# A four-layer recurrent kernel on one core: low-rank and decay products in row and column groups of TensorE, a new order of the pieces, an earlier copy of the values, and a transpose mode

## The chip, the cores and the metric

The kernel runs on one core of one Trainium2 chip. The metric is the device time of one execution in microseconds (us), the median over runs. One profiled execution of the kernel before is shown beside it.

## The reference, cut to what matters

Four layers follow each other. The first three are recurrent layers over 4 sequences of 512 tokens with 512 channels (32 heads of 16); the fourth is an attention over a context of 1024 tokens, which the change does not touch. One recurrent layer computes:

```
xa  = layernorm(x);  sx = shifted(xa) - xa
xxx = tanh((xa + sx*maa_x) @ maa_w1)          # 512 -> 5 streams x 32
xxx = einsum(xxx, maa_w2)                     # each stream: 32 -> 512   ("low-rank products")
xm  = xa + sx*(maa_stack + xxx)               # five mixtures: k, w, v, r, g
w   = exp(-exp(time_decay + tanh(xw @ td_w1) @ td_w2))   # 512 -> 64 -> 512  ("decay products")
r, k, v = xr @ Wr.T, xk @ Wk.T, xv @ Wv.T;  g = silu(xg @ Wg.T)
per token: out = r*(u*k*v + s);  s = k*v + w*s            # 16 x 16 state per head
out = groupnorm(out) * g;  x1 = x + out @ Wo.T
xc  = layernorm(x1); rr = sigmoid(xr2 @ Wfr.T); kk = relu(xk2 @ Wfk.T)**2
x   = x1 + rr * (kk @ Wfv.T)
```

## The kernel before

All values are float32, channels lie on partitions (4 tiles of 128), tokens on the free axis. A unit is one sequence and one half of it: 256 tokens. Each layer has 8 units, so there are 24. The work of a unit is cut in four parts that run in four successive steps: part n (first layernorm, low-rank products, mixtures, projections), part b (the recurrence), part c (output projection, second layernorm) and part e (feed-forward). In step s the engines do part n of unit s+1, b of unit s, c of unit s-1 and e of unit s-2. So there are 27 steps, from -1 to 25. Steps 0 to 22 have both part n and part b, step -1 has only part n, step 23 has b, c and e but no n.

The recurrence works in leaves of 8 tokens. In a leaf, products of pairs of tokens are summed over the channels of a head by a matmul with a block matrix (pieces P0a, P0b, P1, P2a, P2b, P4a to P4d), multiplied by values on VectorE and gathered in o_leaf. Between leaves a scan on VectorE (`scan`) runs over the states; the state updates k x v come from TensorE in 32 x 32 tiles (`updates`, pieces U00 to U13) from keys and values that were turned to lie by token (`keys_by_token` KT0/KT1, `values_by_token` VT0/VT1). The values are then copied by DMA to v_m, spread out for the updates: `load_vm`, four DMAs for pair 0 of the head groups, four for pair 1, in one buffer. The outputs of the states are products in 128 x 32 tiles (`outputs`, `rz` times `s_bd`), added in PSUM to the leaf's own outputs, which `own_outputs` turns (by a matmul with the identity).

Every engine is in order, and its order is written out by hand: one list of calls for each engine and step, which must agree with the lists of PSUM tiles (`A_TILES`, `B_TILES`, `C_TILES`), since a ring of PSUM banks is filled and emptied in that order. The A ring (part n) has three banks, the B ring (part b) two, the outputs one, the C ring (parts c and e) two. A tile can be opened when the tile three (two) places earlier in its ring is emptied by ScalarE or VectorE. SyncE issues `load_vm`, the loads of x and the stores, GpSimd the weights (eight of 1 MB a unit, three slots), each in one fixed order too.

In part n, `lora` computes the five 32-wide streams (a 128-column and a 32-column product), ScalarE takes tanh into th (w, v, r, g in partition groups 0 to 3) and thk (k alone). `lora_pair` issues two streams' products together: each has a contraction of 32 partitions, each its own row group and its own PSUM bank. `lora_k` issues the third stream's alone. `decay_in` and `decay_out` are the two decay products, with 64 output columns and 64 contraction rows. VectorE's `mixing` turns each low-rank product into a mixture with two multiply-adds of 256 tokens, and one addition at its end (mix_w, mix_v, mix_k, mix_r, mix_g). `project` is one half of a 512 x 512 projection: 8 matmuls of 128 x 128 by 256 tokens. Each float32 matmul appears as two records of TensorE in the trace, a transpose as one.

Of the kernel before, what the change touches and what calls it, by code (L numbers as in the profile page):

```python
# [39 lines left out]
W1_AT, W2_AT, W2K_AT, TD1_AT, TD2_AT, SMALL = 0, 640, 1152, 1664, 1920, 2432  # L40
# [7 lines left out]
ROWS_OF = {"w": 0, "v": 1, "r": 2, "g": 3}  # L48
# [45 lines left out]
def other_tiles():  # L94
# [15 lines left out]
A_TILES = [("s1", "act"), ("m1", "dve"), ("s2", "act"), ("i1", "dve"), ("w1", "act"), ("w2w0", "dve"), ("w2v0", "dve"), ("w2w1", "dve"),  # L110
           ("w2v1", "dve"), ("td1", "act"), ("v0", "act"), ("w2k0", "dve"), ("w2k1", "dve"), ("td2_0", "act"), ("td2_1", "act"), ("v1",
           "act"), ("w2r0", "dve"), ("w2g0", "dve"), ("w2r1", "dve"), ("w2g1", "dve"), ("r0", "act"), ("k0", "act"), ("k1", "act"), ("r1",
           "act"), ("g0", "act"), ("g1", "act")]
B_TILES = [("P0a", "dve"), ("P0b", "dve"), ("P1", "dve"), ("P2a", "dve"), ("VT0", "act"), ("VT1", "act"), ("P2b", "dve"), ("P4a", "dve"),
           ("P4b", "dve"), ("P4c", "dve"), ("KT0", "act"), ("KT1", "act"), ("U00", "act"), ("P4d", "dve"), ("U01", "act"), ("U02", "act"),
# [3 lines left out]
C_TILES = [(2, "fr0", "act"), (2, "fk0", "act"), (2, "fk1", "act"), (2, "fr1", "act"), (1, "wo0", "dve"), (2, "fv0", "dve"), (1, "wo1",  # L119
# [5 lines left out]
LEAF_DVE = ["p0", "p1", "u1w", "u1r", "u1k", "p2a", "p2b", "u2w", "u2r", "u2k", "o1", "o2a", "p4a", "p4b", "p4c", "p4d", "u8", "u4r", "u4k",  # L125
# [13 lines left out]
def laid_out():  # L139
# [15 lines left out]
    for i, name in enumerate(("th", "thk", "tdh", "st_a")):  # L155
        at[name] = (at["lm"][0] + TC * i, TC)
# [94 lines left out]
def build(nc, a):  # L251
    ctx = ExitStack()
    with ctx:
# [41 lines left out]
        w2k = small_w[:, W2K_AT:W2K_AT + E]  # L295
# [10 lines left out]
        th, thk, tdh = part_of("th"), part_of("thk"), part_of("tdh")  # L306
# [59 lines left out]
        for _s in range(-1, ITS + 2):  # L366
            weights += [(_it, n) for _it, n in ((_s - 2, WFR), (_s - 2, WFK), (_s - 1, WO), (_s - 2, WFV),
                                                (_s + 1, WV), (_s + 1, WR), (_s + 1, WK), (_s + 1, WG)) if 0 <= _it < ITS]
# [79 lines left out]
        def _(sp):  # L448
# [39 lines left out]
            for s in range(ITS + 2):  # L488
# [3 lines left out]
                if 1 <= n < ITS - 1:  # L492
                    load_xl(n + 1)
                if e >= 0:
                    store_x(e)
                if 0 < b < ITS:
                    load_x1(b)
                if b < ITS:
                    load_vm(b, 1)
                if n < ITS and n % UNITS_PER_LAYER == UNITS_PER_LAYER - 1 and n + 1 < ITS:  # L500
                    sp.wait_ge(a_ring.full, a_ring.full_at(n, "w2g1"))
# [78 lines left out]
        def _(pe):  # L580
# [68 lines left out]
            def lora_k(it):  # L649
                for n in range(2):  # L650
                    t = opened(a_ring, it, f"w2k{n}")
                    for o in range(2):
                        m = 2 * n + o
                        last = mm(t[:, o * TC:(o + 1) * TC], w2k[0:DM, P * m:P * m + P], thk[0:DM, :], start=True, stop=True, skip_group_check=True)
                    a_ring.fill(last, it, f"w2k{n}")

            def lora_pair(it, one, two, n):

                pe.wait_ge(*a_ring.empty_at(it, "w1"))
                t = [opened(a_ring, it, f"w2{s}{n}") for s in (one, two)]  # L660
# [7 lines left out]

            def mixed(it, s):
                return mix[(STREAMS * it + ORDER.index(s)) % 3]  # L670

            def decay_in(it):
                pe.wait_ge(a_dve.sem, a_dve.at(it, "mix_w"))
                t = opened(a_ring, it, "td1")
                for k in range(KT):
                    last = mm(t[0:DD, 0:TC], td1[:, k, :], mixed(it, "w")[:, k, :], start=k == 0, stop=k == KT - 1)  # L676
                a_ring.fill(last, it, "td1")

            def decay_out(it):
                pe.wait_ge(*a_ring.empty_at(it, "td1"))  # L680
                for n in range(2):
                    t = opened(a_ring, it, f"td2_{n}")
                    for o in range(2):
                        m = 2 * n + o
                        last = mm(t[:, o * TC:(o + 1) * TC], td2[0:DD, P * m:P * m + P], tdh[0:DD, :], start=True, stop=True, skip_group_check=True)
                    a_ring.fill(last, it, f"td2_{n}")
# [58 lines left out]
            def own_outputs(it, pair):  # L745
                t = opened(o_ring, it, f"O{pair}").rearrange("p (k s c) -> p k s c", k=2, s=2)
                pe.wait_ge(leaf.sem, leaf.at(it, "o4d"))
                for i in range(2):
                    for s in range(2):
                        mm(t[:, i, s, :], tokens(o_leaf[:, 2 * pair + i, :], s), ident[:], start=i == 0 and s == 0, stop=False, skip_group_check=True)  # L750
# [40 lines left out]
            for s in range(-1, ITS + 2):  # L791
# [5 lines left out]
                if has_b:  # L797
                    products(b, "P0a")
                if 0 < n and has_n:
                    norm_a(n, "s1")  # L800
                if has_b:
                    products(b, "P0b")
                    products(b, "P1")
                if has_e:
                    feed(e, "fk", 1)
                if has_b:
                    products(b, "P2a")
                if 0 < n and has_n:
                    norm_a(n, "m1")
                if has_e:  # L810
                    feed(e, "fr", 1)
                if has_b:
                    values_by_token(b)
                if 0 < n and has_n:
                    norm_a(n, "s2")
                if has_b:
                    products(b, "P2b")
# [4 lines left out]
                if 0 < n and has_n:  # L822
                    norm_a(n, "i1")
                if has_b:
                    products(b, "P4b")
                    products(b, "P4c")
# [1024 lines left out]
```

## Time and profile before

| | us |
|---|---|
| median of 3 runs (3674.37 to 3686.33) | 3674.67 |
| the profiled execution's own time | 3682.92 |
| its span | 3681.2 |
| recurrent part, up to its last product on TensorE | 2635.8 |
| one full step | 102.90 |

The page gives TensorE busy for 94% of the span, VectorE for 72%, ScalarE for 51%. TensorE's busy digit is 9 in every slice from the 4th to the 27th of 40, which is the recurrent part after its first steps. The granted clock is 0.966 of full speed over the whole span. Rows of the trace that follow read: start in us, duration in us, engine and line, xcount for instructions merged into one row, and in brackets the idle time before it and who ended it.

### The profile page before, as it was taken

How to read it: one execution, taken by the hardware profiler on the slowest of the kernel's cores; microseconds unless marked ns; L12 is line 12 of the kernel's file. 1: busy time of each engine (PE TensorE's matmuls, PEld its weight loads, DVE VectorE, ACT ScalarE, POOL GpSimd, SP SyncE). 2: the span in 40 equal slices, each digit the busy share in tenths (PEclk: the TensorE clock that was granted, in tenths of full speed). 3: DMA queues.
4: the chain of work that ended last, by engine and by line, in shares of the span. 5: the costliest groups of instructions: out<-in, count | busy, mean ns of one | idle time of the engine just before them, and what ended most of it. 6: DMA issues, size and time to landing. Idle time of an engine off the chain costs nothing.

```text
span 3681.2 us, 74341 instructions
## 1 busy us (share of the span) xinstructions
PE 3449.4 (94%) x31664; PEld 2579.3 (70%) x31664; DVE 2645.1 (72%) x3721; ACT 1878.6 (51%) x2991; POOL 109.5 (3%) x204
## 2 busy tenths in 40 slices
PE   6889999999999999999999999997588898997998
PEld 4667777777777777777777777775446565565666
DVE  2778887888788888887888888876137466566466
ACT  1455545555555555555555455554146455555555
POOL 1000000000000000000000000000000000000000
PEclk8899999999999999999999999998799899999999
DMA  3113322223233223223233223221323214133222
GB/s 112 44 59 115 115 95 98 99 104 115 87 110 115 104 90 115 98 103 111 86 114 115 104 90 113 101 84 64 139 58 80 83 47 105 47 73 90 48 70 57
DMA packets 91912, 336.61 MB, mean 91 GB/s; under 512 B 16705, under 2 KB 37825, under 8 KB 65601
## 3 DMA queue, kind: packets, MB, share of 16 engines
q0 software_dynamic: 27648, 201.34, 15.1%
q1 hardware_dynamic: 63936, 130.52, 12.3%
q8 instruction: 253, 4.15, 0.5%
q14 instruction: 75, 0.61, 0.1%
HBM read 252.11 MB, written 16.78 MB: 73 GB/s over the span
## 4 chain that ended last, share of the span: by engine, by line
PE 82%; DVE 8%; ACT 3%; SPq 2%; issue 2%; DMA 2%; POOL 0%; ACTq 0%; DVEq 0%; POOLq 0%
PE psum L695 35%; PE psum L704 5%; PE psum L764 4%; PE psum L964 4%; PE psum L741 3%; PE psum L940 3%; PE psum L930 3%; PE psum L665 3%; PE psum L982 2%; PE psum L954 2%; SPq L547 2%; DVE rw L1531 2%; PE psum L945 2%; PE psum L936 2%; PE psum L676 1%
## 5 line engine op out<-in xcount | busy, mean ns | idle before, releaser
L695 PE MATMUL psum<-rw 128*128 128x256 f32 x6144 | 1429.4, 389 | 12.0 <-DVE rw L1369 7.2
L695 PEld LDWEIGHTS psum<-rw 128*128 128x128 f32 x6144 | 1174.8, 194 | 245.6 <-issue 75.2
L1531 DVE TENSOR_TENSOR rw<-rw 128x2048 f32<-128x2048 f32 x192 | 432.6, 2286 | 11.7 <-PE psum L764 11.1
L1707 DVE CUSTOM_DVE_ANT_0 psum<-psum,mem 128x1024 f32<-128x1024 f32 x256 | 313.5, 1225 | 113.9 <-PE psum L954 113.8
L1295 ACT ACTIVATE rest<-psum,mem 128x1024 f32<-128x1024 f32 x256 | 285.0, 1113 | 72.4 <-DVE mem L1707 70.5
L1414 DVE SCALAR_TENSOR_TENSOR rw<-psum,rw 128x256 f32<-128x256 f32 x480 | 199.2, 477 | 153.1 <-PE psum L665 98.6
L1084 ACT ACTIVATE rw<-psum 128x512 f32<-128x512 f32 x192 | 111.8, 595 | 328.6 <-PE psum L695 328.4
L964 PE MATMUL psum<-ident,rest 128*128 128x128 f32 x2048 | 273.2, 277 | 4.0 <-DVE mem L1677 3.8
L1122 ACT ACTIVATE rw<-psum 128x512 f32<-128x512 f32 x192 | 202.1, 1137 | 130.1 <-PE psum L741 128.4
L964 PEld LDWEIGHTS psum<-ident,rest 128*128 128x128 f32 x2048 | 237.4, 142 | 44.1 <-issue 13.5
L954 PE MATMUL psum<-side 128*128 128x512 f32 x512 | 212.0, 495 | 30.2 <-ACT rest L1295 22.7
L704 PE MATMUL psum<-rw 128*128 128x512 f32 x432 | 227.8, 628 | 7.2 <-DVE rw L1447 5.8
L1288 ACT ACTIVATE mem<-psum 128x512 f32<-128x512 f32 x256 | 151.9, 594 | 159.7 <-PE psum L964 159.7
L1501 DVE TENSOR_TENSOR rw<-psum,rw 128x512 f32<-128x512 f32 x168 | 113.5, 687 | 159.6 <-PE psum L704 159.6
L1514 DVE TENSOR_TENSOR_SCAN rw<-rw 128x2112 f32<-128x2112 f32 x48 | 218.5, 4552 | 6.1 <-ACT rw L1122 6.1
L764 PE MATMUL psum<-rw 128*32 128x128 f32 x6144 | 197.4, 278 | 7.0 <-DVE rw L1531 7.0
L1712 DVE COPY mem<-psum 128x512 f32<-128x512 f32 x256 | 175.9, 687 | 36.5 <-PE psum L964 36.4
L1139 ACT ACTIVATE rw<-rw 128x1024 f32<-128x1024 f32 x96 | 192.8, 2010 | 0.0
L764 PEld LDWEIGHTS psum<-rw 128*32 128x32 f32 x6144 | 163.5, 111 | 38.0 <-issue 23.1
L1022 ACT ACTIVATE rw<-rw 128x256 f32<-128x256 f32 x192 | 99.7, 590 | 164.0 <-DVE rw L1364 164.0
L1785 POOL DMA_DIRECT2D rw<-big_dram x192 | 101.0, 528 | 2488.9 <-PE psum L695 2486.2
L741 PE MATMUL psum<-rw 32*32 32x128 f32 x6144 | 167.0, 274 | 6.2 <-DMA rw<-rw 4.6
(147 smaller groups left out, 4503.9 us busy)
## 6 DMA issues: line engine op xcount, KB each, us to landing
rw<-big_dram POOLq DMA_DIRECT2D x192, 1024.0 KB, 5.1
side<-mem SPq DMA_DIRECT2D x256, 128.0 KB, 2.4
rw<-xs_dram SPq DMA_DIRECT2D x32, 512.0 KB, 3.4
side<-mem SPq DMA_DIRECT2D x256, 64.0 KB, 2.0
rw<-rw SPq DMA_DIRECT2D x192, 64.0 KB, 3.1
xs_dram<-rw SPq DMA_DIRECT2D x24, 512.0 KB, 2.7
rw<-x_dram SPq DMA_DIRECT2D x16, 512.0 KB, 3.8
mem<-ctx_dram SPq DMA_DIRECT2D x4, 2048.0 KB, 7.9
```

What stands on the lines that cost most here:

```text
L695: last = mm(t[:, o * TC:(o + 1) * TC], big[:, k, P * m:P * m + P], src[:, k, 0:TC], start=k == 0, stop=k == KT - 1, skip_group_check=True)
L704: b_ring.fill(mm(t, blk, src, start=True, stop=True), it, name)
L741: last = mm(t[32 * g:32 * g + 32, k, :, :, s], k_t[rows, s, 256 * pair + at:256 * pair + at + 32], v_m[rows, s, :, at:at + 32], start=True ...
L764: last = mm(t[32 * q:32 * q + 32, o, s, :], rz[:, k, c, 32 * m:32 * m + 32], s_bd[:, half, NM * i + m, :], start=False, stop=c == 3, skip_ ...
L954: last = mm(t[:, sh, :], q_side[group % 2][:, h, P * q:P * q + P].bitcast(F32R), k_side[group % 2][:, h, sh * 512:sh * 512 + 512].bitcast( ...
L964: last = nc.tensor.transpose(tokens(t, o), tokens(probs[:, n % HPT, :], first + o), ident[:])
L1122: b_ring.empty(f(to, t, ACT.Copy), it, f"U{pair}{q}")
L1295: s_ring.empty(f(probs[:, n % HPT, :].rearrange("p (a s) -> p a s", a=2), s_ring.bank(n, "s"), ACT.Exp, scale=-1.0, bias=mx[:, n % 8:n % 8 ...
L1414: last = stt(to[:, m, :], t[:, o * TC:(o + 1) * TC], par(layer, MAAS, KT * FAN[s] + m), sxa[:, m, :], ALU.add, ALU.mult)
L1514: state_dve.inc(nc.vector.tensor_tensor_scan(s_flat, d_flat, s_flat, 0.0, ALU.mult, ALU.add), it, f"scan{pair}")
L1531: state_dve.inc(tt(s_bd[:, half, :, :].rearrange("p c (h j) -> p c h j", h=4), own, place, ALU.mult), it, f"b{k}{half}")
L1707: maxima.inc(nc.vector.tensor_tensor_reduce(t, t, mbias.rearrange("p (a s) -> p a s", a=2), 1.0, 3.4e38, ALU.add, ALU.min, accum_out=mx[:, ...
```

## The change

It has six parts.

1. Low-rank products: streams w, v and k are issued together in three row groups (`lora_three`), two calls of 6 matmuls; r and g together in two (`lora_two`), two calls of 4. `lora_k` is gone. The stream alone in a tile of its own is now g (thg), not k.
2. Decay: `decay_in` computes the two halves of 128 tokens in two column groups of 64, one bank; `decay_out` computes them in two row groups of 64, a bank each, since td2's rows now lie twice in small_w. ScalarE's exponentials read 8 pieces of 128 tokens where they read 4 of 256.
3. `own_outputs` sets is_transpose on its four matmuls.
4. The order of the pieces on TensorE, VectorE and ScalarE, with the rings' lists.
5. `load_vm` of pair 1 stands ahead of the store of x (`store_x`) and the load of x1 on SyncE.
6. The weights' order is V, K, R, G instead of V, R, K, G; the reload of small_w at a layer's end waits for td2_1 as well.

```diff
-A_TILES = [... ("w1", "act"), ("w2w0", "dve"), ("w2v0", "dve"), ("w2w1", "dve"),
-           ("w2v1", "dve"), ("td1", "act"), ("v0", "act"), ("w2k0", "dve"), ("w2k1", "dve"), ("td2_0", "act"), ("td2_1", "act"), ("v1",
+A_TILES = [... ("w1", "act"), ("w2w0", "dve"), ("w2v0", "dve"), ("w2k0", "dve"),
+           ("w2w1", "dve"), ("w2v1", "dve"), ("w2k1", "dve"), ("v0", "act"), ("td1", "act"), ("v1", "act"), ("td2_0", "act"), ("td2_1",
...
+                if b < ITS:
+                    load_vm(b, 1)
                 if e >= 0:
                     store_x(e)
                 if 0 < b < ITS:
                     load_x1(b)
-                if b < ITS:
-                    load_vm(b, 1)
...
+            def lora_three(it, n):
+                if n == 0:
+                    pe.wait_ge(*a_ring.empty_at(it, "w1"))
+                t = [opened(a_ring, it, f"w2{s}{n}") for s in "wvk"]
                 for o in range(2):
                     m = 2 * n + o
-                    for i, s in enumerate((one, two)):
+                    for i, s in enumerate("wvk"):
                         rows = slice(DM * ROWS_OF[s], DM * ROWS_OF[s] + DM)
                         last = mm(t[i][:, o * TC:(o + 1) * TC], w2[rows, P * m:P * m + P], th[rows, :], ...)
...
             def decay_in(it):
                 for k in range(KT):
-                    last = mm(t[0:DD, 0:TC], td1[:, k, :], mixed(it, "w")[:, k, :], ...)
+                    for h in range(2):
+                        last = mm(t[DD * h:DD * h + DD, 0:P], td1[:, k, :], tokens(mixed(it, "w")[:, k, :], h), ...)
             def decay_out(it):
-                        last = mm(t[:, o * TC:(o + 1) * TC], td2[0:DD, P * m:P * m + P], tdh[0:DD, :], ...)
+                t = [opened(a_ring, it, f"td2_{h}") for h in range(2)]
+                for m in range(KT):
+                    for h in range(2):
+                        rows = slice(DD * h, DD * h + DD)
+                        last = mm(t[h][:, P * m:P * m + P], td2[rows, P * m:P * m + P], tdh[rows, 0:P], ...)
...
-                        mm(t[:, i, s, :], tokens(o_leaf[:, 2 * pair + i, :], s), ident[:], start=i == 0 and s == 0, stop=False, ...)
+                        mm(t[:, i, s, :], tokens(o_leaf[:, 2 * pair + i, :], s), ident[:], start=i == 0 and s == 0, stop=False, is_transpose=True, ...)
...
             def decay_out(it):                                  # ScalarE
-                for n in range(2):
-                    for o in range(2):
-                        last = f(hm["w"][:, 2 * n + o, :], t[:, o * TC:(o + 1) * TC], ACT.Exp, bias=par(layer, TDEC, 2 * n + o))
+                for h in range(2):
+                    for m in range(KT):
+                        last = f(tokens(hm["w"][:, m, :], h), t[:, P * m:P * m + P], ACT.Exp, bias=par(layer, TDEC, m))
```

TensorE's new order in one step, in the names of the calls (o is `own_outputs`, out is `outputs`, U `updates`): fr0 fk0 P0a P0b s1 VT m1 P1 P2a fr1 P2b s2 wo0 P4a i1 fk1 P4b wo1 P4c lora P4d fv0 KT three0 c.s1 o0 U00 U01 three1 U02 U03 fv1 v0 U10 c.m1 U11 decay_in v1 out00 decay_out out01 U12 two0 U13 k0 two1 out10 c.s2 out11 k1 r0 o1 out20 out21 c.i1 r1 out30 out31 g0 g1 N0 N1.

On TensorE, in the middle of part n of a full step, before (L741 updates, L665 `lora_pair`, L676 and L685 decay, L654 `lora_k`, L695 projections):

```order
L665 MATMUL psum<-rw 128x256 x3
L741 MATMUL psum<-rw 32x4x32 [waits b_ring_dve]
L741 MATMUL psum<-rw 32x4x32 x15
L741 MATMUL psum<-rw 32x4x32 [waits b_ring_act]
L741 MATMUL psum<-rw 32x4x32 x15
L695 MATMUL psum<-rw 128x256 [waits c_ring_dve,slot_loaded1,f_act]
L695 MATMUL psum<-rw 128x256 x7
L676 MATMUL psum<-rw 64x256 [waits a_ring_dve,a_dve]
L676 MATMUL psum<-rw 64x256 x3
L695 MATMUL psum<-rw 128x256 [waits a_ring_dve,slot_loaded2,a_dve]
L695 MATMUL psum<-rw 128x256 x7
L654 MATMUL psum<-rw 128x256 [waits a_ring_dve]
```

The same place of the changed kernel (L750 updates, L659 `lora_three`, L683 and L693 decay, L704 projections, L773 outputs, L620 the second norm's mean):

```order
L659 MATMUL psum<-rw 128x256 x5
L750 MATMUL psum<-rw 32x4x32 [waits b_ring_act]
L750 MATMUL psum<-rw 32x4x32 x15
L750 MATMUL psum<-rw 32x4x32 [waits b_ring_act]
L750 MATMUL psum<-rw 32x4x32 x15
L704 MATMUL psum<-rw 128x256 [waits c_ring_dve,slot_loaded1,f_act]
L704 MATMUL psum<-rw 128x256 x7
L704 MATMUL psum<-rw 128x256 [waits a_ring_dve,slot_loaded2,a_dve]
L704 MATMUL psum<-rw 128x256 x7
L750 MATMUL psum<-rw 32x4x32 [waits b_ring_act,vm_loaded]
L750 MATMUL psum<-rw 32x4x32 x15
L620 MATMUL psum<-rw 128x256 [waits c_ring_act]
```

The first value projection v0 now follows fv1 directly, the first update of pair 1 (which waits for vm_loaded) comes right behind it, and the decay products come later, with 8 matmuls of 128 tokens each.

On SyncE in an early step before (L483 `load_vm`, L463 load of x for part n, L473 `store_x`, L469 load of x1):

```order
L483 DMA rw<-rw 32x2x256 [waits b_ring_full,b_ring_act]
L483 DMA rw<-rw 32x2x256 x3
L463 DMA rw<-x_dram 128x1024 [waits a_act]
L473 DMA xs_dram<-rw 128x1024 [waits f_dve]
L469 DMA rw<-x_dram 128x1024 [waits x_stored]
L483 DMA rw<-rw 32x2x256 [waits b_ring_full]
L483 DMA rw<-rw 32x2x256 x3
```

and in the changed kernel:

```order
L483 DMA rw<-rw 32x2x256 [waits b_ring_full,b_ring_act]
L483 DMA rw<-rw 32x2x256 x3
L463 DMA rw<-x_dram 128x1024 [waits a_act]
L483 DMA rw<-rw 32x2x256 [waits b_ring_full]
L483 DMA rw<-rw 32x2x256 x3
L473 DMA xs_dram<-rw 128x1024 [waits f_dve]
L469 DMA rw<-x_dram 128x1024 [waits x_stored]
```

The four copies of pair 1 no longer stand behind the store, which waits for VectorE (f_dve), and behind the load that waits for that store.

## Rows read from the trace of the kernel before

**Rows 1.** The page, part 1: busy time, share and instructions of each engine.

```profile
PE 3449.4 (94%) x31664; PEld 2579.3 (70%) x31664; DVE 2645.1 (72%) x3721; ACT 1878.6 (51%) x2991; POOL 109.5 (3%) x204
```

**Rows 2.** Windows: stretch, its length, busy us of each engine, clock, DMA.

```profile
1404.97:1507.87 102.90, 102.68 (x999) 80.58 (x999) 85.52 (x112) 55.35 (x84) 4.20 (x8) 1.00 0.29 103
```

**Rows 3.** Chain that ended last, one full step: start us, us to next.

```profile
1415.65 0.95 PE psum L750 x8
1416.60 1.88 PE psum L764 x64
...
1450.44 0.87 PE psum L718 x8
1451.32 0.58 PE psum L603 x32
...
1452.96 3.45 PE psum L695 x16
1456.41 0.86 PE psum L704 x2
1457.27 0.84 PE psum L608 x8
...
1471.23 1.01 PE psum L741 x32
...
1473.29 1.06 PE psum L665 x8
...
1476.99 1.49 PE psum L741 x64
1478.49 3.65 PE psum L695 x16
1482.14 1.87 PE psum L676 x8
...
1487.66 1.92 PE psum L654 x8
1489.58 1.92 PE psum L685 x8
...
1496.21 1.09 PE psum L750 x8
```

**Rows 4.** Timeline of VectorE in the same step.

```profile
1429.57 3.25 DVE L1369 SCALAR_TENSOR_TENSOR rw<-rw 128x256 f32<-128x256 f32 x8
...
1473.33 0.69 DVE L1501 TENSOR_TENSOR rw<-psum,rw 128x512 f32<-128x512 f32 x1 [5.64 <-PE psum L704]
...
1477.03 1.66 DVE L1414 SCALAR_TENSOR_TENSOR rw<-psum,rw 128x256 f32<-128x256 f32 x4 [0.88 <-PE psum L665]
1478.60 2.35 DVE L1419 TENSOR_TENSOR rw<-rw 128x1024 f32<-128x1024 f32 x2
1480.87 4.55 DVE L1514 TENSOR_TENSOR_SCAN rw<-rw 128x2112 f32<-128x2112 f32 x1
...
1491.69 4.49 DVE L1531 TENSOR_TENSOR rw<-rw 128x2048 f32<-128x2048 f32 x2
```

**Rows 5.** Timeline of ScalarE: a copy of states, and the decay's exponentials.

```profile
1488.19 1.98 ACT L1139 ACTIVATE rw<-rw 128x1024 f32<-128x1024 f32 x1
1490.73 1.64 ACT L1066 ACTIVATE rw<-psum,rw 128x256 f32<-128x256 f32 x4 [0.57 <-PE psum L685]
```

**Rows 6.** Timeline of SyncE's queue in the same step.

```profile
1487.35 0.33 SPq L473 DMA_DIRECT2D xs_dram<-rw  x1
1490.01 0.32 SPq L469 DMA_DIRECT2D rw<-xs_dram  x1
1490.38 2.52 SPq L483 DMA_DIRECT2D rw<-rw  x4
```

**Rows 7.** The page, part 6: the copies of `load_vm`, count, KB each, us to landing.

```profile
rw<-rw SPq DMA_DIRECT2D x192, 64.0 KB, 3.1
```

**Rows 8.** TensorE's timeline in step 23.

```profile
2530.53 2.81 PE L741 MATMUL psum<-rw 32*32 32x128 f32 x64 [4.59 <-DMA rw<-rw]
```

More of the change, by code:

```diff
@@ L680, in decay_out @@
                 pe.wait_ge(*a_ring.empty_at(it, "td1"))
[L681 to L686, printed above, removed]
+                t = [opened(a_ring, it, f"td2_{h}") for h in range(2)]
+                for m in range(KT):
+                    for h in range(2):
+                        rows = slice(DD * h, DD * h + DD)
+                        last = mm(t[h][:, P * m:P * m + P], td2[rows, P * m:P * m + P], tdh[rows, 0:P], start=True, stop=True, skip_group_check=True)
+                        if m == KT - 1:
+                            a_ring.fill(last, it, f"td2_{h}")
             def project(it, n, tiles, name, key, src):
@@ L749, in own_outputs @@
                     for s in range(2):
-                        mm(t[:, i, s, :], tokens(o_leaf[:, 2 * pair + i, :], s), ident[:], start=i == 0 and s == 0, stop=False, skip_group_check=True)
+                        mm(t[:, i, s, :], tokens(o_leaf[:, 2 * pair + i, :], s), ident[:], start=i == 0 and s == 0, stop=False, is_transpose=True, skip_group_check=True)
             def outputs(it, k, half):
@@ L798, in _ @@
                     products(b, "P0a")
+                    products(b, "P0b")
                 if 0 < n and has_n:
@@ L801, in _ @@
                 if has_b:
[L802 to L807, printed above, removed]
+                    values_by_token(b)
                 if 0 < n and has_n:
                     norm_a(n, "m1")
+                if has_b:
+                    products(b, "P1")
+                    products(b, "P2a")
                 if has_e:
@@ L835, in _ @@
                 if has_b:
-                    updates(b, 0, 0)
                     products(b, "P4d")
+                if has_e:
+                    feed(e, "fv", 0)
+                if has_b:
+                    keys_by_token(b)
                 if has_n:
-                    lora_pair(n, "w", "v", 0)
+                    lora_three(n, 0)
                 if has_c:
@@ L842, in _ @@
                 if has_b:
+                    own_outputs(b, 0)
+                    updates(b, 0, 0)
                     updates(b, 0, 1)
                 if has_n:
-                    lora_pair(n, "w", "v", 1)
+                    lora_three(n, 1)
                 if has_b:
@@ L851, in _ @@
                 if has_n:
-                    decay_in(n)
                     stream(n, "v", 0)
-                    lora_k(n)
-                    decay_out(n)
-                    stream(n, "v", 1)
-                    lora_pair(n, "r", "g", 0)
-                if has_b:
-                    own_outputs(b, 0)
-                    outputs(b, 0, 0)
-                if has_n:
-                    lora_pair(n, "r", "g", 1)
                 if has_b:
                     updates(b, 1, 0)
-                    updates(b, 1, 1)
                 if has_c:
@@ L1193, in _ @@
                     scan_inputs(b, 0)
+                if has_e:
+                    feed(e, "fk", 1)
+                if has_n:
+                    lora(n)
+                if has_b:
                     by_token(b, "KT0", k_t)
@@ new lines, in mixing @@
+                if n == 0:
+                    for s in streams:
+                        turn = STREAMS * it + ORDER.index(s)
+                        if turn >= 3:
+                            old_it, old = (turn - 3) // STREAMS, ORDER[(turn - 3) % STREAMS]
+                            dve.wait_ge(a_ring.full, a_ring.full_at(old_it, "td1" if old == "w" else old + "1"))
+                        if it and ORDER.index(s) < 3:
+                            dve.wait_ge(b_ring.full, b_ring.full_at(it - 1, "P4d"))
@@ new lines, in mixing, with mixed @@
+                for s in streams:
+                    t = filled(a_ring, it, f"w2{s}{n}")
+                    to = mix[(STREAMS * it + ORDER.index(s)) % 3]
+                    for o in range(2):
+                        m = 2 * n + o
+                        last = stt(to[:, m, :], t[:, o * TC:(o + 1) * TC], par(layer, MAAS, KT * FAN[s] + m), sxa[:, m, :], ALU.add, ALU.mult)
+                    a_ring.empty(last, it, f"w2{s}{n}")
+            def mixed(it, s):
+                to = mix[(STREAMS * it + ORDER.index(s)) % 3]
+                dve.wait_ge(*a_ring.empty_at(it, f"w2{s}1"))
+                a_dve.inc(tt(to, to, xa_a[:, :, PAD:PAD + TC], ALU.add), it, "mix_" + s)
@@ L1585, in _ @@
                     level2(b)
+                if 0 < n and has_n:
+                    norm_a(n, "m1")
+                if has_b:
                     values(b, "P1", 0, 1, 0)
@@ L1597, in _ @@
                 if has_b:
-                    gather(b, "P2b", "o2b", 0, 2)
+                    gather(b, "P2a", "o2a", 1, 2)
+                if 0 < n and has_n:
+                    norm_a(n, "xn")
+                if has_b:
+                    values(b, "P2b", 0, 2, 1)
                     values(b, "P4a", 1, 4, 0)
```

215 lines of the change are left out of this document (105 added, 110 removed).

## The prediction

> **What bounds the kernel now.** I read the page first, then one full step in the windows view, then the chain that ended last over the same step, then VectorE's and ScalarE's timelines there. TensorE is busy for 94% of the span [rows 1], and in a full recurrent step for 102.68 of 102.90 us at full clock, with VectorE at 85.52 and ScalarE at 55.35 [rows 2]. The chain of that step is one TensorE piece behind the other [rows 3]. So in the recurrent part a microsecond taken off TensorE is a microsecond off the time, as long as VectorE, which has 17.4 us to spare in a step, still hands everything over in time in the new order. The attention part is not touched.
>
> **The change, part by part, for one full step on TensorE.** All from [rows 3].
>
> Own outputs. Two groups of four identity matmuls, eight records each, 1.09 and 0.95 us. As transposes they have one record each. The eight transposes of `values_by_token` take 0.87 us, 0.109 each, so four take 0.44 instead of the 0.87 that stands in the 0.95 and 1.09 after the cost of a changed tile. Twice 0.5: -1.0 us. The accumulation behind them is the same.
>
> Low-rank products. Removed: `lora_k` 1.92 and four `lora_pair` of 1.06, 6.16 us. A pair has four matmuls of 256 tokens and takes 1.06, the four of `lora_k` alone 1.92: two row groups run fully side by side. Added: two calls with three row groups and two pairs. The pairs stay at 1.06. For three groups no row stands here. Lower end: the same 1.06, if the third group is as free as the second. Upper end: 12 weight loads of 128 columns one behind another. Four matmuls of only 64 tokens (L608), but with 128 columns of weights, take 0.84 for eight records, 0.105 each, as long as ones of 128 tokens: there the load sets the pace. 12 x 0.105 + 0.2 = 1.5. I take 1.10: -1.85, at the upper end -1.05.
>
> Decay. Removed 1.87 + 1.92 = 3.79. `decay_in` becomes four pairs of 128 tokens in two column groups. Half of the tokens, half of the time: (1.87 - 0.16)/2 + 0.2 = 1.05. The outputs' 128 x 32 tiles do the like (32 records in 1.01). `decay_out` has the same pairs in row groups, but with 16 loads of 128 columns: 1.05 if those run side by side, 16 x 0.105 + 0.2 = 1.9, no gain, if they don't. I take 1.05 for both: -1.7, at the upper end -0.85.
>
> New order. A lone `updates` takes 1.01, two in a row 1.49. Before there are three such couples and two alone, after two couples and four alone: 2 x 1.49 + 4 x 1.01 = 7.02 against 6.49, +0.5. A projection behind another kind of tile takes 3.65, one behind 128 x 128 work 3.45. v0 now follows fv1 and r0 follows k1: -0.4. The 0.22 us of waiting [rows 2] sits at the second norm's sums, which now lie in the middle of the outputs and later than ScalarE needs: -0.2.
>
> Sum: -1.0 - 1.85 - 1.7 + 0.5 - 0.4 - 0.2 = -4.65, a step of 98.3. With the loads one behind another it is 1.65 longer, 99.9.
>
> **What might be late in that step.** I laid the new list out with these durations from the step's start: fr0 fk0 to 6.9, P0b 8.7, P2a 12.4, fr1 15.9, wo0 21.0, fk1 26.1, wo1 30.4, `lora` 34.9, P4d 36.0, fv0 39.5, three0 41.5, U01 44.2, three1 45.3, U03 46.8, fv1 50.4, U11 56.6, v1 61.3, out01 64.4, U13 67.6, k0 71.3, out11 74.7, k1 78.4, r0 81.8, out21 84.2, r1 88.5, out31 90.4, g1 97.4, N1 98.3. On VectorE four multiply-adds go in 1.57, an addition in 1.14, the scan in 4.5, two blocks in 4.5 [rows 4]. The tight places are these.
> - v0 needs mix_v. three0 ends at 41.5, six multiply-adds take 2.4 (43.9, and three1 needs that at 44.2); three1 ends 45.3, 2.4 more, two additions 2.3: 50.0 against 50.4.
> - The first r, g product needs td2_0 empty. ScalarE's four exponentials of 256 tokens take 1.64 [rows 5]; eight of 128 should take about 2.4, +0.8 us on ScalarE, which has 47 to spare. td2_0 is free at about 65.4, and it is needed at 65.4.
> - U10 needs the copies of pair 1. SyncE issues them at U03's end, 46.8; four issues take 2.5 [rows 6], the last lands 3.1 later [rows 7], about 52.3, needed at 53.9. Before they were issued behind the store and the load, 3.0 us after the store [rows 6]. The wait for U03 that now stands ahead of the store holds nothing: the store is ready at 57. So part 5 gives nothing by itself in a full step; it lets U10 stand where it does. If it were late by 1 us, that is 1 us a step.
> - g0 needs mix_g: the blocks end 87.8, then the norm's product 1.2 and an addition 1.15 give 90.15 against 90.4.
> - fr0 of the next step needs mixr: eight multiply-adds take 3.25 for both mixtures [rows 4]; mixr is there at 97.5 against 98.3.
> VectorE's longest stand before, 5.64 us for P4d behind `lora` and the updates [rows 4], is split: 2.3 for P4d, 1.5 for fv0. It fits, but at five places with less than 1 us. I add 0.5 us a step for what these layouts leave out (semaphores' latencies): 98.8, -4.15.
>
> **Steps.** 22 full steps (1 to 22): -91. Step 0 has the same parts, partly at a lower clock and with waits: -3. Step -1: -2. Step 23 has the own outputs' gain and the 4.59 us that TensorE waited for the copies [rows 8], which are no longer behind the store: -4, since scan1 behind them sets the end. Together -100; I take 98, since the waits of step 0 mostly stay. The profiled execution itself took 3682.9 us (span 3681.2 and 1.7 around it), so 3585 by its own clock. The median of the runs is 8 us lower than that execution: 3674.7 - 98 = 3577.
>
> The page "TensorE: Matmul & The Clock Gate" of the Trainium skill, section "LDWEIGHTS (loading the stationary operand)", says that a load's time goes by the columns of the weights and not by their rows. That speaks against this change: a tile of 32 or 64 rows would save nothing on its loads. By it, if loads also queue, it is rival 1. The same page's "The mechanism" says that a load overlaps running matmuls where the row groups differ; by that it is the forecast. The 0.84 of the 64-token matmuls agrees with the first, and no row here decides whether two loads of 128 columns run at once: the pair's 1.06 is what both give.
>
> **Rivals.**
> 1. Loads of 128 columns queue even across row groups. For: 0.105 a record at 64 tokens, and a pair's eight records at 0.107 each. Against: two updates in a row issue 64 records in 1.49, 0.023 each, with 32 columns, which by 0.105 for 128 columns would be 0.026 each, 1.68. Price: 1.65 x 23 = 38 us, 3615.
> 2. VectorE gets a little late at two or three of the tight places, 1 to 2 us a step beyond my 0.5. For: five margins under 1 us, and three mixtures now stand ahead of scan0, with the copies, states and outputs behind it. Against: VectorE has 12.8 us free in a step of 98.3. 1.5 x 23 = 35 us, 3612.
> 3. Slower: the loop of scan0, states, blocks, outputs, group mean and mixtures on VectorE becomes the bound. It decides from where VectorE's forced standing in a step exceeds 17.4 us (before it stood 17.4 with TensorE full); my layout has it at 12.8. A delay of 7 us in this loop (scan0 held behind two multiply-add groups, both additions and one late U03) gives 85.5 + 20 = 105.5 a step, +60: 3735. It needs a chain of misses in my layout, each ten times the margins' size.
> 4. It doesn't do what it says: transposes in an accumulating bank or column groups in one bank run one behind another. The outputs' 32 records in 1.01 use four column groups in one bank side by side, so only the transposes are open: +1 us a step, 3600.
>
> **Chances.** Forecast 0.55, rival 1 0.18, rival 2 0.12, rival 4 0.03, rival 3 0.05; 0.07 for little or no net gain, from rivals 1 and 2 together and worse. The forecast's own range is 3558 to 3598: without any new wait the sum is 3674.7 - 22 x 4.65 - 9 = 3563, and 5 us are for the rounded pieces. The range that holds 8 in 10 reaches over rivals 1 and 2, and as far below 3563: 3552 to 3630. A measurement of this kernel can tell 0.5% (18 us) from no change. Faster by over 0.5%: 0.87. Within 0.5%: 0.07. Slower: 0.06.
>
> **What would show it.** In the changed profile a full step should be 98 to 99 us long with TensorE still over 99% busy. The four transposes of `own_outputs` should have four records and take about 0.45 to 0.6; `lora_three` 12 records in 1.1 (1.5 by rival 1); `decay_in` 16 records in 1.05; `decay_out` 16 records in 1.05 (1.9 by rival 1). ScalarE's exponentials should take 0.3 each. Waits of TensorE for VectorE's additions (mix_v, mix_g) or mixr above 1 us a step would show rival 2, a VectorE near 90% of a step rival 3. The forecast is wrong if the step is not between 97.5 and 99.3 us, or if the attention part behind it moves.

## The result and the profile after

The changed kernel takes 3555.75 us (median of 4 runs, 3551.16 to 3556.6) against 3676.53 for the kernel before in the same series. The ratio is 0.9664, 95% interval 0.965 to 0.9677: 121 us faster, where 98 were forecast. That is 21 us below the forecast of 3577 and 2 below the forecast's own range (3558 to 3598), but inside the wide one (3552 to 3630). The profiled execution took 3555.04 us, its span 3553.2.

The windows view of one full step of the changed kernel (stretch, length, busy us of TensorE, weight loads, VectorE, ScalarE, GpSimd, then the granted clock, the DMA engines' busy share and GB/s), to be read beside [rows 2]:

```profile
1454.90:1553.23 98.33, 98.27 (x1008) 77.99 (x1007) 84.97 (x112) 54.51 (x87) 4.23 (x8) 1.00 0.34 121
```

The step went from 102.90 to 98.33 us, 4.57 less (4.65 in the sum of the pieces, 4.15 with the waits that were added to it). TensorE is still busy without a gap; VectorE does the same 85 us.

The chain that ended last over that step (start us, us to the next piece), the lines that answer to [rows 3]:

```profile
1495.41 0.87 PE psum L727 x8
1496.28 1.07 PE psum L659 x12
1497.35 0.57 PE psum L598 x8
1497.92 0.59 PE psum L759 x4
1498.51 1.49 PE psum L750 x64
...
1502.75 7.10 PE psum L704 x32
1509.85 1.01 PE psum L750 x32
1510.86 0.63 PE psum L620 x2
1511.49 1.01 PE psum L750 x32
1512.49 1.02 PE psum L683 x16
...
1518.18 1.09 PE psum L693 x16
...
1537.50 0.44 PE psum L759 x4
```

- `own_outputs` (L759) has four records in 0.59 and 0.44 us, where it had eight in 1.09 and 0.95.
- `lora_three` (L659) issues three streams in 1.07, as long as `lora_pair` took for two (1.06). A pair itself still takes 1.06: in TensorE's timeline `lora_two` begins at 1521.22 and the next piece at 1522.28.
- `decay_in` (L683) takes 1.02 for 1.87, `decay_out` (L693) 1.09 for 1.92.
- A lone `updates` (L750) still takes 1.01; the couple in the rows above takes 1.49.
- fv1 and v0 in a row (L704 x32) take 7.10 where two apart took 7.30.

VectorE's and ScalarE's timelines of the same step at the tight places, and SyncE's queue one step earlier (start, duration, idle time in brackets):

```profile
1503.56 2.35 DVE L1435 TENSOR_TENSOR rw<-rw 128x1024 f32<-128x1024 f32 x2
...
1524.77 4.56 DVE L1530 TENSOR_TENSOR_SCAN rw<-rw 128x2112 f32<-128x2112 f32 x1 [0.39 <-ACT rw L1134]
...
1544.73 1.22 DVE L1435 TENSOR_TENSOR rw<-rw 128x1024 f32<-128x1024 f32 x1
```

```profile
1519.55 2.15 ACT L1078 ACTIVATE rw<-psum,rw 128x128 f32<-128x128 f32 x8
```

```profile
1402.79 2.92 SPq L483 DMA_DIRECT2D rw<-rw  x4
...
1412.83 0.33 SPq L473 DMA_DIRECT2D xs_dram<-rw  x1
1415.49 0.33 SPq L469 DMA_DIRECT2D rw<-xs_dram  x1
```

The mixtures w and v are done at 1505.9, and v0 begins half way through the 7.10 us of L704, at 1506.3. mix_g is done at 1545.95, and g0 begins at 1546.25. Four of the eight exponentials have emptied td2_0 at 1520.7, and `lora_two` needs it at 1521.2. So the margins of 0.4 and 0.25 us that were laid out are really there, 0.5 stands where none was left for td2_0, and all hold. The eight exponentials take 2.15 us (2.4 were assumed). The copies of pair 1 (L483) go out right behind U03, 10 us ahead of the store (L473).

**Where the 128 us between the two profiled spans lie.** The steps' lengths are read from one start of the transposes at a step's end (N0) to the next in TensorE's timeline. In steps 2 to 22, 21 times 4.57: 96.0. Step 1: 6.9. Steps -1 and 0: 14.0. Step 23: 6.6. In some steps the granted clock falls to half for a few microseconds (a dip), and these steps are longer: four by 5.0 and two by 1.7 us before, eight by 1.7 and one by 3.3 after, 6.6 less in all. What follows the last N0 is 2 longer. The attention part alone, from the last product of the recurrent part on, went from 1045.4 to 1048.3.

### The profile page after: what moved, and what is told of

Same layout as the page of the kernel before. It is cut to its first block, busy times and chain, and to the rows that moved or that the text cites. A ratio compares the mean times of both kernels' runs of the same rounds, so it can differ in the third digit from the quotient of the medians.

```text
span 3553.2 us, 74824 instructions
## 1 busy us (share of the span) xinstructions
PE 3326.4 (94%) x31856; PEld 2507.2 (71%) x31856; DVE 2632.3 (74%) x3721; ACT 1861.2 (52%) x3087; POOL 109.9 (3%) x204
## 4 chain that ended last, share of the span: by engine, by line
PE 86%; DVE 6%; ACT 3%; SPq 2%; DMA 2%; issue 1%; POOL 0%; ACTq 0%; DVEq 0%; POOLq 0%
PE psum L704 39%; PE psum L713 5%; PE psum L773 5%; PE psum L750 4%; PE psum L976 4%; PE psum L952 3%; PE psum L942 3%; PE psum L994 3%; PE psum L966 2%; SPq L548 2%; PE psum L957 2%; PE psum L948 2%; PE psum L659 2%; DVE psum L1734 1%; PE psum L669 1%; PE psum L609 1%
## 5 line engine op out<-in xcount | busy, mean ns | idle before, releaser
L704 PE MATMUL psum<-rw 128*128 128x256 f32 x6144 | 1421.7, 388 | 19.5 <-DVE rw L1435 10.6
L704 PEld LDWEIGHTS psum<-rw 128*128 128x128 f32 x6144 | 1172.8, 194 | 234.5 <-issue 52.8
L773 PE MATMUL psum<-rw 128*32 128x128 f32 x6144 | 200.2, 277 | 6.1 <-DVE rw L1547 6.1
L773 PEld LDWEIGHTS psum<-rw 128*32 128x32 f32 x6144 | 161.4, 111 | 37.8 <-issue 17.4
L750 PE MATMUL psum<-rw 32*32 32x128 f32 x6144 | 180.8, 274 | 1.2 <-ACT rw L1134 1.2
L750 PEld LDWEIGHTS psum<-rw 32*32 32x32 f32 x6144 | 142.0, 105 | 41.4 <-issue 39.1
```

Source lines behind the costliest of these rows:

```text
L704: last = mm(t[:, o * TC:(o + 1) * TC], big[:, k, P * m:P * m + P], src[:, k, 0:TC], start=k == 0, stop=k == KT - 1, skip_group_check=True)
L750: last = mm(t[32 * g:32 * g + 32, k, :, :, s], k_t[rows, s, 256 * pair + at:256 * pair + at + 32], v_m[rows, s, :, at:at + 32], start=True ...
L773: last = mm(t[32 * q:32 * q + 32, o, s, :], rz[:, k, c, 32 * m:32 * m + 32], s_bd[:, half, NM * i + m, :], start=False, stop=c == 3, skip_ ...
```

## The experiments

All changes of a step below are for steps in which the clock did not fall ("undisturbed"). "Changed kernel" is the kernel after, at 98.33 us a step and a ratio of 0.9664 to the kernel before; the times of a run are compared by their ratio to the kernel before on the same chip.

### The transposes: taken out of the changed kernel (a_plain_own), alone in the one before (b_turned_own)

```diff
-... start=i == 0 and s == 0, stop=False, is_transpose=True, skip_group_check=True)
+... start=i == 0 and s == 0, stop=False, skip_group_check=True)
```

> The changed kernel with own_outputs as plain identity matmuls again (no transpose mode). Theory (a plain product costs two records, a transpose one): each group of four goes back from 0.44-0.59 to 0.95-1.09 us, +1.0 us a full step, +23 to +25 us over the kernel, so about 3580. Rival (the mode makes no difference to matmuls in an accumulating bank, or VectorE's loop hides it): within 5 us of the changed kernel's 3556.

Measured: 3562.16 us, ratio 0.968 (0.9667 to 0.9693), about 6 us over the changed kernel. But the step is 99.30, +0.97, as the theory says: L759 is back at eight records.

```profile
1207.99 1.16 PE L759 MATMUL psum<-ident,rw 128*128 128x128 f32 x8
1247.99 1.05 PE L759 MATMUL psum<-ident,rw 128*128 128x128 f32 x8
```

22 steps of 0.97 are 21 us. In the profile three steps are longer by 1.7 us because of the clock, against nine in the changed kernel, which is 12 of it given back and leaves 9; the medians show 6, the two profiled executions 13 (step 1 alone is 3.0 longer). So the rival (no difference) is refuted for the pieces, and the size expected in the time was wrong: the transposes make each step 0.97 shorter, and the steps with a dip are more in the profile with them. That they cause the dips is not shown, and the next run speaks against it.

The same edit alone in the kernel before:

> The kernel before with only the transpose mode of own_outputs. Theory of the step: 102.90 less 0.97 = 101.9 us where no dip of the clock falls in; that is -21 over 22 steps, -24 with the others. In the changed kernel the plain form cost 0.97 a step but took six dips of 1.7 us out of the profile, so the theory of the clock (less of TensorE's work in a step brings more dips) expects more or longer dips here than the seven steps of before, and a time of -12 to -24. Rival (dips fall at random): -24 within 3.

Measured: 3659.86 us, ratio 0.9944 (0.9929 to 0.996), 19 us faster than the kernel before. The undisturbed step is 102.31, only 0.59 less. TensorE's timeline of that step shows a wait that the kernel before did not have there:

```profile
1296.85 1.08 PE L764 MATMUL psum<-rw 128*32 128x128 f32 x32 [0.21 <-DVE rw L1531]
```

In the old order TensorE now arrives at out21 before VectorE's blocks (L1531) are ready, and the couple of outputs is split. The theory of the step (101.9) was wrong; that the time, -19, lies in its range all the same is luck. The longer steps were 5 in this profile, by 1.6 or 3.3 us, 13 us together, against six (not seven, as the expectation says) and 23 before: the theory of the clock expected more, and this run does not bear it out.

### The decay products: whole in the changed kernel (a_decay_whole), in groups in the one before (b_decay_groups)

In the changed kernel, the four edits on TensorE and ScalarE taken back (`decay_in` and `decay_out` on each; the first is shown):

```diff
-                    for h in range(2):
-                        last = mm(t[DD * h:DD * h + DD, 0:P], td1[:, k, :], tokens(mixed(it, "w")[:, k, :], h), ...)
+                    last = mm(t[0:DD, 0:TC], td1[:, k, :], mixed(it, "w")[:, k, :], ...)
...
```

> The changed kernel with the decay products in their old form (four matmuls of 256 tokens each, one column group, one row group), at the new places. Theory (groups run side by side): decay_in goes from 1.02 back to 1.87, decay_out from 1.09 to 1.92, +1.68 us a full step, +39 us, and if the single-group pieces also bring back the longer dips of the granted clock, up to 10 us more: 3595 to 3605. Rival (VectorE's loop has slack of under 1 us, so TensorE's extra time is partly hidden): +20.

Measured: 3583.39 us, ratio 0.9741 (0.9728 to 0.9754), 28 us over the changed kernel. The undisturbed step is 100.00, +1.67, the theory's 1.68. No step shows a hiding of the extra time in VectorE's loop, so the rival's reason is wrong, though its +20 is nearer to the time than the theory's +39: the clock fell in six steps, five by 1.7 and one by 3.3, 12 us, against 17 for the changed kernel. The two profiled spans are 29 us apart: 35 for steps 2 to 22 and 4 for step 1, less 5 for the clock in full steps, 2 for steps -1, 0 and 23, and 3 behind the last N0. The clock did not bring the 5 us steps back, so that part of the expectation is wrong too.

In the kernel before:

> The kernel before with only the decay products in groups, at their old places. Theory (the groups' gain is a matter of the pieces, not of the new order): the undisturbed step goes from 102.90 to 101.2 (-1.68), -39 us; the dip of 6.8 us at half clock that falls behind lora_k and decay_out in five steps of before should go or shrink with that stretch (14 us more at most). 3630 to 3645. Rival (the old order makes decay_out wait for ScalarE's tanh, which starts later relative to the shorter pieces): a wait of 0.3 to 0.8 us a step at decay_out or v1, 101.5 to 102.

Measured: 3641.41 us, ratio 0.9896 (0.988 to 0.9911), 38 us faster than before. The undisturbed step is 101.58, 1.32 less instead of 1.68, and the rival's wait is there:

```profile
1258.94 1.99 PE L655 MATMUL psum<-rw 32*128 32x256 f32 x8
1261.22 1.16 PE L688 MATMUL psum<-rw 64*128 64x128 f32 x16 [0.29 <-DVE rw L1418]
```

It is VectorE's low-rank multiply-adds (L1418), not ScalarE's tanh, that decay_out waits for: its second bank held a tile of `lora_k`. The loss is 0.36 us a step, of which this row shows 0.29. The steps of 107.9 (four in the profile before, where the expectation says five) are gone here; half of the steps are longer by 1.7.

### The three parts together, in the old order (b_three_parts)

The transposes, the decay groups and the early copies, with the old low-rank products.

> The kernel before, in its old order, with the transposes, the decay groups and the early copies together; only the low-rank products and the order are old. Alone they took 0.59 and 1.32 us off the step, where the pieces themselves got 0.97 and 1.68 shorter. Theory (VectorE's loop begins to bind in the old order): together they give less than the sum of 1.91, a step of 101.2 to 101.5 and 3630 to 3640. Rival (the lost part is a fixed wait each): 102.90 - 1.91 = 100.99, 3625.

Measured: 3625.8 us, ratio 0.9858 (0.9842 to 0.9875), undisturbed step 101.00. The rival is right and my theory wrong: 102.90 less 0.59 less 1.32 is 100.99. Both waits stand in this run's step, with the lengths that they had alone (0.29 and 0.21):

```profile
1356.63 1.16 PE L688 MATMUL psum<-rw 64*128 64x128 f32 x16 [0.30 <-DVE rw L1418]
...
1386.01 1.08 PE L768 MATMUL psum<-rw 128*32 128x128 f32 x32 [0.21 <-DVE rw L1535]
```

VectorE's loop does not bind more when both are in; each part loses its own fixed wait.

### The changed kernel without transposes and decay groups (a_order_lora)

> The changed kernel with plain own_outputs and whole decay products: only the new order, the low-rank groups and the early copies are left of the change. Theory (TensorE's pieces add up): 98.33 + 0.97 + 1.67 = 100.97 us a step, 1.93 below the kernel before, which is the low-rank products' 1.85 and next to nothing from the order itself; 3556 + 59 less a few dips, 3600 to 3612. Rival (the order's slack is used up and pieces overlap VectorE's waits): 100.5 or less.

Measured: 3607.57 us, ratio 0.9807 (0.9792 to 0.9821), undisturbed step 100.98, as the theory has it (100.97), with TensorE busy throughout:

```profile
1389.90:1490.88 100.98, 100.98 (x1000) 79.77 (x999) 85.40 (x113) 54.18 (x83) 4.22 (x8) 1.00 0.30 105
```

So of the 4.57 us the order, the low-rank products and the early copies together bring 1.92, the decay groups 1.67 and the transposes 0.97. By the pieces, the low-rank products account for 6.16 - 2 x 1.07 - 2 x 1.06 = 1.90 of the 1.92. This leaves next to nothing to the order by itself; what it does is let 0.97 and 1.67 through where the old order let 0.59 and 1.32 through. What the low-rank groups would give in the old order was not run, so their share is read from the pieces and not from a run without them.

### The place of the copies (a_copy_late, b_copy_early)

Behind the store and the load of x1 again, in the changed kernel:

```diff
-                if b < ITS:
-                    load_vm(b, 1)
                 if e >= 0:
                     store_x(e)
                 if 0 < b < ITS:
                     load_x1(b)
+                if b < ITS:
+                    load_vm(b, 1)
```

> The changed kernel with the copies of pair 1 behind the store and the load of x1 on SyncE again. Theory (the early copy is what lets U10 stand behind v0): the store is ready about 57 us into the step, the load follows 2.7 later, the four issues take 2.5 and land 1.9 after: about 64.5, while U10 stands at 54: TensorE waits about 10 us a step for a DMA, partly given back since VectorE catches up; +150 to +230 us, about 3700 to 3790, slower than the kernel before. Rival (the copies' place matters in step 23 only): +5, 3561.

Measured: 3852.29 us, ratio 1.0465 (1.0451 to 1.048), 296 us over the changed kernel and more than was expected. A step is 112.65. SyncE's queue and TensorE's timeline in one step:

```profile
1221.62 0.33 SPq L473 DMA_DIRECT2D xs_dram<-rw  x1
1224.28 0.32 SPq L469 DMA_DIRECT2D rw<-xs_dram  x1
1224.64 2.52 SPq L483 DMA_DIRECT2D rw<-rw  x4
```

```profile
1228.57 1.93 PE L750 MATMUL psum<-rw 32*32 32x128 f32 x32 [9.95 <-DMA rw<-rw]
1235.35 4.91 PE L704 MATMUL psum<-rw 128*128 128x256 f32 x16
```

```profile
1163.64:1276.29 112.65, 102.64 (x1008) 80.91 (x1007) 85.10 (x112) 54.44 (x87) 4.22 (x8) 0.92 0.27 94
```

TensorE stands 9.95 us for the copies, and nothing of it is caught up. The other 4.4 us are the clock: it was granted at 0.92 over the step, and the pieces behind the stand are slower (the first update's row takes 1.93 where it takes 1.08 in the changed kernel's timeline). The expectation had the wait right. It missed the clock, and it expected part of the wait to be given back, which did not happen.

Ahead of the store, alone in the kernel before:

> The kernel before with only the copies of pair 1 ahead of the store. Theory (the place on SyncE counts only where TensorE would use it): a full step stays 102.90 us, step 23 loses the 4.59 us wait for the copies: -3 to -5 us against the kernel before, about 3674 of 3678. Rival (copies that land early move VectorE and ScalarE ahead): steps below 102.8, -20 us or more.

Measured: 3677.08 us, ratio 0.9996 (0.9986 to 1.0005), full steps of 102.90, step 23 86.46 instead of 90.88. The theory holds: -4.4 us in step 23, nothing in a full step. The early copy is worth nothing that can be measured alone, and 296 us with the order that rests on it.

### The order of the matmuls in three row groups (a_streams_in_turn)

```diff
-                for o in range(2):
-                    m = 2 * n + o
-                    for i, s in enumerate("wvk"):
+                for i, s in enumerate("wvk"):
+                    rows = slice(DM * ROWS_OF[s], DM * ROWS_OF[s] + DM)
+                    for o in range(2):
```

> The changed kernel with lora_three's six matmuls stream by stream (w w v v k k) instead of turn by turn (w v k w v k). Theory (matmuls start in program order, so two of one row group hold back the next group's): w1 overlaps v0 and v1 overlaps k0, 4 x 0.43 + 0.2 = 1.9 instead of 1.07 us a call, two calls, +1.7 us a step, +39 us, 3595. Rival (each row group takes its own matmuls from a queue, whatever the order): no change, 3556.

Measured: 3555.58 us, ratio 0.9662 (0.9649 to 0.9675), undisturbed step 98.34. The rival is right:

```profile
1301.03 1.15 PE L659 MATMUL psum<-rw 32*128 32x256 f32 x12
1302.11 0.64 PE L598 MATMUL psum<-rw,ones 128*32 128x256 f32 x8
```

12 records in 1.08 us, whether the streams take turns or not. Two matmuls of one row group in a row do not hold up the next group's. The single records say the same. In program order the stream w is finished with its fourth record, which signals that its bank is full. In this trace the three records that carry such a signal are the last three to start, at 1301.779, 1301.792 and 1301.806, so the three row groups advanced side by side.

### A version that beats both (a_side_by_side)

```diff
-                if has_b:
-                    updates(b, 1, 0)
                 if has_c:
                     norm_c(c, "m1")
                 if has_b:
+                    updates(b, 1, 0)
                     updates(b, 1, 1)
                 if has_n:
                     decay_in(n)
                     stream(n, "v", 1)
+                    decay_out(n)
                 if has_b:
                     outputs(b, 0, 0)
-                if has_n:
-                    decay_out(n)
-                if has_b:
                     outputs(b, 0, 1)
                     updates(b, 1, 2)
+                    updates(b, 1, 3)
                 if has_n:
                     lora_two(n, 0)
-                if has_b:
-                    updates(b, 1, 3)
```

> The changed kernel with U10 and U11 in a row again, U12 and U13 in a row, the second norm's mean ahead of U10, and decay_out ahead of both outputs. TensorE's pieces then take 1.0 to 1.3 us a step less (two lone updates become one couple twice, 0.5 each, and fewer changes of tile). Theory (VectorE's loop has 0.9 us to spare: mixr is ready 0.9 before fr0, mix_g 0.3 before g0): TensorE begins to wait for VectorE at g0 and fr0, the step falls to between 97.4 and 97.9, -10 to -20 us, 3536 to 3546. Rival 1 (VectorE's own waits of 0.39 and 0.84 shrink along): step 97.1, -27. Rival 2 (two0 now comes behind four updates and delays the r and g mixtures): mix_g late, step 98.3 or more, no gain.

Measured: 3526.86 us, ratio 0.9584 (0.9568 to 0.9599), 29 us faster than the changed kernel and 152 faster than the one before. The undisturbed step is 97.49, in the theory's range; the time is 9 us below the theory's 3536 to 3546. The step's 0.84 makes 18 of the 29 us, the rest is the clock, which fell in two steps that are 3.3 us longer each (7 us against 17). TensorE's busy time in the step fell by 1.16 us, as expected, and VectorE's loop now shows:

```profile
1242.93:1340.42 97.49, 97.11 (x1007) 77.47 (x1006) 84.98 (x113) 54.44 (x87) 4.22 (x8) 1.00 0.30 109
```

```profile
1298.29 1.56 PE L750 MATMUL psum<-rw 32*32 32x128 f32 x64
...
1325.97 1.08 PE L773 MATMUL psum<-rw 128*32 128x128 f32 x32 [0.32 <-DVE rw L1543]
```

The wait is at out21, for VectorE's blocks, and not at g0 and fr0 where I expected it. From `lora_three`'s second call to the last blocks VectorE stands only once, 0.32 us:

```profile
1291.63 2.35 DVE L1431 TENSOR_TENSOR rw<-rw 128x1024 f32<-128x1024 f32 x2
1293.90 4.55 DVE L1526 TENSOR_TENSOR_SCAN rw<-rw 128x2112 f32<-128x2112 f32 x1
...
1306.76 4.49 DVE L1543 TENSOR_TENSOR rw<-rw 128x2048 f32<-128x2048 f32 x2 [0.32 <-PE psum L773]
...
1321.43 4.48 DVE L1543 TENSOR_TENSOR rw<-rw 128x2048 f32<-128x2048 f32 x2
```

So the next microsecond has to come off VectorE between three1 and out21, or be moved out of there.

## Why the prediction was right, and where its sizes were off

**What bounds.** Right. TensorE's sum of pieces is the length of a full step: a_plain_own (99.30) and a_decay_whole (100.00) give 0.97 and 1.67 for the two parts, and a_order_lora, which lacks both, has 100.98 where 98.33 + 0.97 + 1.67 is 100.97.

**The pieces.** Own outputs: -1.0 forecast, 0.97 measured by taking it out. Decay: -1.7 forecast, 1.67 measured. Low-rank: -1.85 forecast, 1.90 by the pieces. A step of 98.3 was the sum; 98.33 came. For updates, projections and the lost wait the forecast had -0.1 in total (+0.5 - 0.4 - 0.2), and a_order_lora leaves 1.92 for them and the low-rank products together. The step's own sign (98 to 99 us, TensorE over 99% busy) came true with 98.33 and 98.27 busy.

**What the step had to wait for.** I added 0.5 us a step for waits that the layout leaves out. There were none: TensorE is busy for 98.27 of 98.33. This is the first term mis-sized, 22 x 0.5 = 11 us. The margins came out as they were laid out from rows taken start to start, so nothing had to be added for latencies.

**The edges.** Steps -1, 0, 1 and 23 were forecast at -2, -3, -4.15 and -4, and brought 14.0 (the first two), 6.9 and 6.6: 27.5 for 13.15, 14 us more. This is the second term mis-sized. In step 23 the gain is the copies' 4.4 (b_copy_early) and 2 for the other parts. In the profiled execution of before, steps -1 and 0 ended at 187.0 us. In b_copy_early, which has the same pieces on TensorE there, they ended at 182.95, and its granted clock from 100 to 150 us is 0.83 against 0.76. So some 4 of the 14 us are the clock of that one execution. The other 10, where 5 were forecast, were not taken apart: the clock is below full in both kernels up to 150 us (0.93, 0.86, 0.76 before and 0.90, 0.96, 0.77 after, in stretches of 50 us), TensorE waits for other engines there, and the prediction took most of these waits to stay.

**The clock.** Not in the sum. The steps with a fallen clock cost 6.6 us less in the changed profile. Against that, the profiled execution of before was 6.4 us above its median, which the forecast took out.

**The sum.** From 98 forecast to 128 between the profiled executions: 2 that the forecast took off its own 100, 11 for the waits, 14 for the edges, 7 for the clock, less 2 for pieces (21 x 0.08) and 2 behind the last N0. The medians are 121 apart, since the execution of before was 6.4 above its median and the one after 0.7 below.

One sign of being wrong was that the attention part moves. It did so by 2.9 us of 1045, with the clock at its lower level for 102.4 us of it after and 99.0 before, by which I estimate 1.7 of the 2.9.

**Rival 1, the loads of 128 columns.** Refuted. Twelve records with such loads take 1.07 us, 0.089 each, sixteen take 1.09, 0.068 each, where 0.105 was the pace of the 64-token matmuls [rows 3]. The 0.84 us of those is a pace within one tile. Of the Trainium skill's "TensorE: Matmul & The Clock Gate", its section "LDWEIGHTS (loading the stationary operand)" (time by columns, whatever the rows) speaks of one load, which no run here timed alone, and says nothing of two in different row groups; "The mechanism", by which loads overlap running matmuls of other row groups, agrees with these traces (1.07 us for three row groups, 1.06 for two). The same section says that matmuls themselves begin and end strictly in program order. a_streams_in_turn does not fit that: by my estimate the order w w v v k k would then have cost 0.86 us a call (four matmuls of 0.43, an eighth of the 3.45 of a half projection, behind each other instead of two), and it cost 0.01.

**Rivals 2 to 4.** VectorE was not late at the tight places of the new order; their margins came out at 0.4 (mix_v), 0.5 (td2_0), 0.3 (mix_g) and 0.7 us (mixr). Rival 3 did not happen. Rival 4 is refuted by L759's four records in 0.44, and for the column groups by `decay_in`'s 1.02.

**Part 5.** "Gives nothing by itself in a full step" was right (102.90 with it alone), and so was that it carries the place of U10; late copies cost 9.95 us a step plus 4.4 for the clock.

## What to carry to other kernels

Where one engine is busy without a gap for a whole stage, add its pieces up from start to start, lay the new order out with the other engines' hand-over times beside it, and trust the sum: it needed no allowance here. Packing small matmuls into row and column groups paid its full arithmetic, but only in an order that put other work between a piece and the engine that empties its bank; in the old order the decay groups lost a fifth of their gain to a new wait, and the transposes two fifths. A copy that is issued early can be worth nothing alone and be the condition for an order, so it has to be tested in both.

## What the runs showed of the hardware that was not expected

**TensorE's clock fell although TensorE was never idle, at the same places of the step each time.** In the changed kernel the windows view of a stretch in which the clock fell shows 0.80, with TensorE busy all the time:

```profile
1402.80:1411.30 8.50, 8.50 (x32) 7.00 (x32) 8.50 (x7) 1.51 (x2) 0.53 (x1) 0.80 0.30 85
```

It comes right behind the small tiles from three0 to U03, and fv1 and v0 take 8.8 us for 7.1 there. Four of the nine dips of this profile lie at this place, 47 to 48 us behind N0. The other five lie 68.6 to 68.9 us behind it, as k0 begins, behind the small tiles from out00 to U13. One of them:

```profile
433.60:436.80 3.20, 3.20 (x9) 2.54 (x8) 2.83 (x3) 1.90 (x3) 0.00 (x0) 0.50 0.00 0
```

In the kernel before, six dips lie behind the updates that precede fv1, and in four of these steps a longer one follows in `decay_out`, the level of 1.2 GHz nearly throughout:

```profile
554.90:561.70 6.80, 6.80 (x17) 4.96 (x17) 5.20 (x3) 2.50 (x5) 0.00 (x0) 0.52 0.19 68
```

Ahead of it TensorE had worked for some 3 us with one row group of 32 (`lora_k`) and then one of 64 partitions. The steps that are 5 us longer are the ones with both dips, 1.7 and 3.3. They came only in the kernel before and in the one with early copies alone (b_copy_early; a_copy_late, where the clock is low for 14 to 17 us of every full step, is left aside). In b_turned_own, which has that stretch unchanged, the long dip came three times without the one ahead of it. In the two old-order runs with the decay in groups it never came there. Over the runs the dips cost 5 us (plain outputs), 12 (whole decay), 17 (changed kernel) and 7 us (side by side), for nearly the same work, so a difference of 10 us between two versions can be the clock alone. What decides in which steps it falls was not settled.

**Row groups take their matmuls independently of the order between them.** Shown above for three row groups: 1.08 us with the streams one behind another against 1.07 in turns.
